# Reordering the hand-written end of the attention and giving the 1024-wide weights a fifth flag

## The reference

```python
x = x + attn(layernorm(x))
x = x + xattn(layernorm(x), ctx, ctx, mask)
h = silu(h_in @ w1.T * s1) * (h_in @ w2.T * s2)      # h_in = layernorm(x), 256 -> 1024
h = gelu(h @ h1.T * s_h1)                            # 1024 -> 1024
h = gelu(h @ h2.T * s_h2)                            # 1024 -> 1024
x = x + h @ w3.T * s3                                # 1024 -> 256
```

## Time and profile before

| What | Value |
|---|---|
| median of 3 runs | 1508.51 us (1506.88 to 1509.42) |
| profiled execution, its own time | 1507.81 us |
| its span in the trace | 1506.0 us |
| mean granted TensorE clock | 0.999 |
| PE busy | 1487.9 us, 99% |
| DVE, ACT, POOL busy | 1101.3, 968.6, 492.1 us |

### The profile page before, as it was taken

The page is one execution under the profiler, slowest core; times in us unless marked ns, Lnnn a source line. Parts: engine busy times, 40 slices in busy tenths (PEclk is TensorE's granted clock), DMA queues, the critical chain, the costliest instruction groups (busy, mean ns, idle before and its releaser), DMA issues.

```text
span 1506.0 us, 29162 instructions
## 1 busy us (share of the span) xinstructions
PE 1487.9 (99%) x10680; PEld 1262.7 (84%) x10680; DVE 1101.3 (73%) x2772; ACT 968.6 (64%) x2274; POOL 492.1 (33%) x763
## 2 busy tenths in 40 slices
PE   8999999999999999999998999999999999999999
PEld 6888888888888888888887788888888888888887
DVE  7999999999999899999999657555553634444443
ACT  6888888888888888888887754456444532222222
POOL 2545454445544555454453011000110212221110
PEclk9999999999999999999999999999999999999999
DMA  4000000000000000000013423421212632222221
GB/s 155 2 1 2 30 2 30 1 2 30 2 29 1 2 30 1 16 15 2 22 64 113 145 84 113 150 103 66 79 66 78 215 114 85 84 85 84 85 84 43
DMA packets 56024, 87.15 MB, mean 58 GB/s; under 512 B 4416, under 2 KB 33472, under 8 KB 55872
## 3 DMA queue, kind: packets, MB, share of 16 engines
q1 hardware_dynamic: 55872, 85.10, 16.5%
HBM read 55.72 MB, written 29.36 MB: 56 GB/s over the span
## 4 chain that ended last, share of the span: by engine, by line
PE 91%; DVE 5%; ACT 2%; DMA 1%; issue 1%; POOL 0%; SPq 0%; DVEq 0%
PE bank L1024 15%; PE bank L1026 13%; PE bank L658 10%; PE bank L578 9%; PE bank L630 8%; PE bank L580 7%; PE bank L579 7%; PE bank L642 6%; PE bank L1179 2%; PE bank L1170 2%; PE bank L1032 2%; PE bank L1146 2%; PE bank L1138 2%; PE bank L1139 2%; PE bank L1140 2%
## 5 line engine op out<-in xcount | busy, mean ns | idle before, releaser
L844 POOL TENSOR_SCALAR P<-P,stats 128x512 f32<-128x512 f32 (+3 forms) x512 | 269.0, 544 | 376.4 <-DVE stats L822 376.1
L717 ACT ACTIVATE P<-P,stats 128x384 f32<-128x384 f32 (+3 forms) x512 | 283.9, 560 | 16.4 <-DVE stats L814 16.2
L681 ACT ACTIVATE PT<-bank 128x512 fp32r<-128x512 f32 (+1 forms) x384 | 185.4, 525 | 87.6 <-PE bank L642 86.5
L814 DVE CUSTOM_DVE_ANT_0 P<-bank,cmask 128x384 f32<-128x384 f32 (+3 forms) x512 | 228.4, 483 | 1.2 <-PE bank L630 0.9
L731 DVE TENSOR_TENSOR PT<-bank,PT 128x512 fp32r<-128x512 f32 (+1 forms) x384 | 218.8, 594 | 5.3 <-ACT PT L681 4.1
L1336 DVE TENSOR_TENSOR Hb<-gt,Hb 128x512 fp32r<-128x512 f32 x128 | 90.8, 710 | 167.0 <-ACT Hb L1187 165.9
L1024 PE MATMUL bank<-Hb,hw 128*128 128x512 f32 x512 | 202.3, 395 | 0.8 <-DVE Hb L1336 0.8
L1024 PE MATMUL bank<-w,hw 128*128 128x512 f32 x512 | 199.2, 389 | 0.0
L658 PEld LDWEIGHTS bank<-PT,V 128*128 128x128 f32 x1024 | 165.0, 190 | 22.1 <-DVE PT L731 4.3
L658 PE MATMUL bank<-PT,V 128*128 128x512 f32 (+3 forms) x1024 | 176.7, 320 | 3.5 <-DVE PT L731 3.5
L1026 PE MATMUL bank<-Hb,hw 128*128 128x512 f32 x448 | 174.8, 390 | 0.0
(11 more groups left out here) (230 smaller groups left out, 3305.4 us busy)
## 6 DMA issues: line engine op xcount, KB each, us to landing
h_scratch<-go SPq DMA_DIRECT2D x64, 256.0 KB, 2.0
xs<-x_scratch SPq DMA_DIRECT2D x23, 512.0 KB, 4.1
hx<-h_scratch SPq DMA_DIRECT2D x32, 256.0 KB, 6.1
stageA<-in_h SPq DMA_DIRECT2D x14, 512.0 KB, 3.6
x_scratch<-x SPq DMA_DIRECT2D x8, 512.0 KB, 3.0
x_scratch<-xs SPq DMA_DIRECT2D x8, 512.0 KB, 2.9
qf<-h_scratch SPq DMA_DIRECT2D x16, 256.0 KB, 5.3
pf<-h_scratch SPq DMA_DIRECT2D x16, 256.0 KB, 6.0
```

Source lines behind the costliest of these rows:

```text
L681: return e.activation(dst, src, ACT.Copy, scale=scale)
L717: e.activation(p, p, ACT.Exp, bias=st_[:, k:k + 1], scale=-1.0, accum_out=st_[:, 8 + k:9 + k]).then_inc(s_exp, 1)
L814: e.tensor_tensor_reduce(P_tile(P, i, a), banks["S", P, max(i, 1)][a][:, slice(*S_COLS[i])], cmask[:, 512 - n:512], -1.0, 3.0e38, ALU.add, ...
L844: e.tensor_scalar(p, p, stats[P % 4][:, k:k + 1], 1.0, ALU.mult, ALU.mult).then_inc(s_norm, 1)
```

## The change

- In TAIL the ends of the five lists are reordered. PE does `g.0.0` to `u.0.2` ahead of `O.63` and `O.64`. DVE does `pl.63.2.0` and `os.62` ahead of `xoa`, `lnorm.1.0` earlier, and `fl.12` after `hl.0.7`. ACT does `big.12` and `fh.13` to `fh.16` after `hh.0.7`. SP issues `xload.1` after `ld.9` and `ld.14` after `ld.12`.
- There is a flag 4. Flag 3 covers pieces 5 to 10, flag 4 pieces 5 to 12 and is loaded in `h.0.2`; `ft.4` and `fm.4` follow `h.0.1`.
- The row of flag 2 is transposed and loaded after the first three matmuls of both `g.0.0` and `u.0.0`; their last matmuls follow then.
- A gated tile waits for the high parts of XTs ahead of its first two matmuls, for the first low part ahead of the third, and for the second low part ahead of the fourth.

```diff
 "PE"
-        T.63.1 O.62 xo.0.0 xo.0.1 AV.63.0 AV.63.1 xv.2 xv.3 xt.0.1.0 xt.0.1.1 ft.2 O.63 O.64 g.0.0 u.0.0 g.0.1
-        u.0.1 g.0.2 u.0.2 g.0.3 u.0.3 g.0.4 u.0.4 g.0.5 u.0.5 g.0.6 u.0.6 g.0.7 u.0.7 ft.3""",
+        T.63.1 O.62 xo.0.0 xo.0.1 AV.63.0 AV.63.1 xv.2 xv.3 xt.0.1.0 xt.0.1.1 ft.2 g.0.0 u.0.0 g.0.1 u.0.1 g.0.2
+        u.0.2 O.63 O.64 g.0.3 u.0.3 g.0.4 u.0.4 g.0.5 u.0.5 g.0.6 u.0.6 g.0.7 u.0.7 ft.3""",
 "ACT"
-        ph.63.0.1 ph.63.1.0 ph.63.1.1 ph.63.2.0 fh.7 fh.8 big.7 yo.63.0 fh.9 yo.63.1 big.8 xvh.2 fh.10 xvh.3
-        xth.0.1.0 xth.0.1.1 big.9 fh.11 big.10 silu.0.0 silu.0.1 big.11 silu.0.2 hh.0.1 silu.0.3 hh.0.3 silu.0.4
-        fh.12 silu.0.5 fh.13 fh.14 big.12 hh.0.5 silu.0.6 silu.0.7 fh.15 hh.0.6 hh.0.7 fh.16 big.13 big.14""",
+        ph.63.0.1 ph.63.1.0 ph.63.1.1 ph.63.2.0 fh.7 fh.8 yo.63.0 yo.63.1 fh.9 big.7 xth.0.1.0 xth.0.1.1 big.8
+        xvh.2 silu.0.0 xvh.3 fh.10 silu.0.1 big.9 silu.0.2 hh.0.1 fh.11 silu.0.3 big.10 hh.0.3 silu.0.4 silu.0.5
+        hh.0.5 big.11 silu.0.6 fh.12 silu.0.7 hh.0.6 hh.0.7 big.12 fh.13 fh.14 fh.15 fh.16 big.13 big.14""",
 "DVE"
-        xvl.1 xr.0 ys.62.1 pl.63.0.0 pl.63.2.1 xpl.0 pl.63.0.1 pl.63.1.0 pl.63.1.1 xoa.0.0 os.62 fl.7 pl.63.2.0
-        xoa.0.1 lsum.0.1 ys.63.0 fl.8 xva.2 ys.63.1 lnorm.0.1 xva.3 flag.2 fl.9 xtl.0.1.0 xtl.0.1.1 fl.10 fm.2
-        fl.11 xvl.2 xvl.3 os.63 os.64 hm.0.0 hm.0.1 hl.0.0 hm.0.2 hl.0.1 hm.0.3 hl.0.2 hl.0.3 hm.0.4 fl.12
-        hl.0.4 hm.0.5 lsum.1.0 flag.3 hl.0.5 fm.3 hm.0.6 hm.0.7 lnorm.1.0 hl.0.6 hl.0.7 fl.13 fl.14 fl.15 fl.16""",
+        xvl.1 xr.0 ys.62.1 pl.63.0.0 pl.63.2.1 xpl.0 pl.63.0.1 pl.63.1.0 pl.63.1.1 pl.63.2.0 os.62 xoa.0.0
+        xoa.0.1 lsum.0.1 fl.7 ys.63.0 lnorm.0.1 fl.8 xtl.0.1.0 xtl.0.1.1 xva.2 flag.2 xva.3 fm.2 ys.63.1 fl.9
+        hm.0.0 xvl.2 xvl.3 hm.0.1 hl.0.0 fl.10 hm.0.2 hl.0.1 os.63 os.64 lsum.1.0 hm.0.3 hl.0.2 hl.0.3 fl.11
+        hm.0.4 hl.0.4 hm.0.5 lnorm.1.0 hl.0.5 flag.3 fm.3 hm.0.6 hl.0.6 hm.0.7 hl.0.7 fl.12 flag.4 fl.13 fl.14
+        fl.15 fl.16""",
 "POOL"
-        n.63.1.0 yh.62 yl.62 lpow.0.1 yh.63 yl.63 hh.0.0 hh.0.2 hh.0.4 lpow.1.0""",
+        n.63.1.0 yh.62 yl.62 lpow.0.1 yh.63 yl.63 hh.0.0 hh.0.2 lpow.1.0 hh.0.4""",
 "SP"
-        xload.0 st.6 mb ld.0 ld.1 ld.2 ld.3 ld.6 ld.5 ld.4 ld.7 ld.8 ld.9 ld.10 ld.11 ld.13 ld.14 st.7 ld.12
-        ld.15 xload.1 ld.16""",
+        xload.0 st.6 mb ld.0 ld.1 ld.2 ld.3 ld.6 ld.5 ld.4 ld.7 ld.8 ld.9 xload.1 ld.10 ld.11 ld.13 st.7 ld.12
+        ld.14 ld.15 ld.16""",
...
-                o += [("h", 0, 1)] + also(0, ("h", 1)) + [("gelu", 0, 1), ("hst", 0, 1), ("big", 16)]
+                o += [("h", 0, 1), ("ft", 4), ("fm", 4)] + also(0, ("h", 1)) + [("gelu", 0, 1), ("hst", 0, 1), ("big", 16)]
...
-    FLAGS = (2, 3, 0, 1)
-    LOOKED = {2: 4, 3: 8, 0: 12}
+    FLAGS = (2, 3, 4, 0, 1)
+    LOOKED = {2: 4, 3: 6, 4: 8, 0: 12}
...
+        def gated(kind, m, out, ready):
+
+            W, ms = w1 if kind == "g" else w2, slice(m * 128, m * 128 + 128)
+            w.wait_ge(s_x2hi, ready)
+            e.matmul(out[:, :], W[:, 0, 0, ms], XTs[:, 0, 0, :], start=True, stop=False)
+            e.matmul(out[:, :], W[:, 0, 1, ms], XTs[:, 0, 1, :], start=False, stop=False)
+            w.wait_ge(s_x2lo, ready - 1)
+            e.matmul(out[:, :], W[:, 0, 0, ms], XTs[:, 1, 0, :], start=False, stop=False)
+
+        def gated_rest(kind, m, out, ready):
+            W, ms = w1 if kind == "g" else w2, slice(m * 128, m * 128 + 128)
+            with e.If_ne(low, 0):
+                for c in range(2):
+                    e.matmul(out[:, :], W[:, 1, c, ms], XTs[:, 0, c, :], start=False, stop=False)
+            w.wait_ge(s_x2lo, ready)
+            e.matmul(out[:, :], W[:, 0, 1, ms], XTs[:, 1, 1, :], start=False, stop=True).then_inc(s_gu, 1)
...
-                if item == ("g", 0, 0):
-                    look_up(2)
...
+                gated(kind, m, out, xt_at(b, 1))
+                if item == ("u", 0, 0):
+                    flag_row(2)
+                    look_up(2)
+                    gated_rest("g", m, bank["g", 0, 0], xt_at(b, 1))
+                if item != ("g", 0, 0):
+                    gated_rest(kind, m, out, xt_at(b, 1))
...
-                       {(0, 0): 3, (0, 4): 0}.get((b, m)), ...
+                       {(0, 0): 3, (0, 2): 4, (0, 4): 0}.get((b, m)), ...
```

More of the change, by code:

```diff
@@ L356, in program @@
     st = at(1.21875, "st0", [128, 12])
-    flags = at(1.28125, "flags", [128, 8])
+    flags = at(1.28125, "flags", [128, 10])
     rmax = [at(1.375 + 0.0625 * i, f"rmax{i}", [128, 16]) for i in range(2)]
@@ L1008, in look_up, with flag_row @@
             e.reg_load(low, flags[0:1, 2 * k + 1:2 * k + 2].bitcast(i32))
+        def flag_row(k):
+            out, = claim(w, ("ft", k))
+            w.wait_ge(s_found, FLAGS.index(k) + 1)
+            e.transpose(out[0:1, 0:128], flags[:, 2 * k:2 * k + 1], ident[:, :]).then_inc(s_ft, 1)
+        def gated(kind, m, out, ready):
[12 more added lines that the diff above has]
+            e.matmul(out[:, :], W[:, 0, 1, ms], XTs[:, 1, 1, :], start=False, stop=True).then_inc(s_gu, 1)
         def scores_by_rows(b):
@@ L1123, in pe_rest @@
                 i.then_inc(s_xo, 1)
[L1124 to L1127, removed]
+            elif kind == "ft" and a[0] != 2:
+                flag_row(a[0])
             elif kind == "use":
@@ L1131, in pe_rest @@
                 b, m = a
-                ms = slice(m * 128, m * 128 + 128)
                 out, = claim(w, item)
[L1134 to L1140, removed]
-                if item == ("g", 0, 0):
+                for q in split_done(W1 if kind == "g" else W2):
+                    w.wait_ge(*q)
+                gated(kind, m, out, xt_at(b, 1))
+                if item == ("u", 0, 0):
+                    flag_row(2)
                     look_up(2)
[L1143 to L1146, removed]
+                    gated_rest("g", m, bank["g", 0, 0], xt_at(b, 1))
+                if item != ("g", 0, 0):
+                    gated_rest(kind, m, out, xt_at(b, 1))
             elif kind == "h":
@@ L1153, in pe_rest @@
                 hidden(out, lambda i, c: Hb[c][:, i, :], m, lambda c: (s_hlo, 8 * b + c + 1),
-                       {(0, 0): 3, (0, 4): 0}.get((b, m)), b + 1 if m == (2 if b == 0 else 1) and b + 1 < B else 0).then_inc(s_hid, 1)
+                       {(0, 0): 3, (0, 2): 4, (0, 4): 0}.get((b, m)), b + 1 if m == (2 if b == 0 else 1) and b + 1 < B else 0).then_inc(s_hid, 1)
             elif kind == "gh":
```

## The result

Five executions of each kernel on one chip: 1514.77 us (median; 1514.64 to 1516.89) after, 1506.88 us (1506.43 to 1509.42) before; ratio 1.0051 [1.0036, 1.0065]. The change makes the kernel slower, by 7.9 us between the medians. The profiled execution of after took 1516.89 us with a span of 1515.1. The forecast of 1514.6 lies closer to the median than its sum does: it was 6.1 us on top of 1508.51, the median of three, and five executions put before at 1506.88. That it hits the median within 0.2 us is luck: the base was 1.6 us too high and the sum 1.8 too low.

What follows compares the result with a forecast made beforehand. PE, busy 99% of the span, was taken to bound the kernel. Terms of +4.5 (xs.1), +0.3 (look-up), +1.8 (half clock) and -0.5 (wait) gave +6.1 us, 1514.6 as a median; range 1509.5 to 1519.

Steps and rivals of the forecast that it cites:

- Steps 1 and 2: Handover and first gated tiles: xt 4.2 us early, g.0.0 at 815.7, then 1.3 us lost at flag 2's row.
- step 1: Handover from AV.63 to xt: AV.63 starts 2.5 us earlier at full clock, and xt starts 4.2 us early.
- Step 3: At ft.3, which waits for flag.3 on DVE: ft.3 comes at 836.5, 1.5 us early.
- Step 4: From ft.3 to xs.1: ACT's and DVE's chain takes 16.3 us, so PE waits about 5.5 us ahead of xs.1.
- Step 5: The rest: look-up 0.3 us, half clock at the xs.1 gap 1.8, a later wait of 0.5 gone.
- The look-up in h.0.2: Loading the new flag within h.0.2 costs 0.3 us, as the one in h.0.0 did.
- The 0.5 us wait of the earlier trace: PE's largest wait after 857 us goes, as later batches' gated tiles start on the high parts: 0.5 us gained.
- The sum: Whole kernel: +4.5 at xs.1, +0.3 look-up, +1.8 half clock, -0.5 wait, together 6.1 us slower.
- That ACT catches up: Rival at xs.1: xtl.1.0.1 ends before about 847.5, so the kernel is about 3 us faster, 1505.3; chance 0.14.
- No change: Rival: the gap ahead of xs.1 is half as long and the clock stays up, +1 to +3 us; chance 0.14.
- That the clock falls in the handover too: Rival: gaps from 812.3 to 818.5 bring another half clock, another 1.8 us partly hidden, 1516; chance 0.12.

Runs made afterwards that it cites:

- e2_late: The kernel after with ACT's and DVE's weight pieces 12 to 14 and lnorm.1.0 put about where before had them; 1510.05 us, ratio to before 1.0012.
- e3_code: All five lists of the kernel before with the code of the kernel after, flag.4 the only item added; 1507.41 us, ratio to before 0.9997.
- b6: b2 with the flag's register load moved two steps earlier in the hidden tile; 1504.32 us, ratio to before 0.9975.
- b3: The kernel before, its code, flags and PE list kept, with ACT's, DVE's and SP's lists reordered; 1507.16 us, ratio to before 0.9993.
- d1_pieces: The kernel after with fh.13 and fh.14 moved ahead of big.12 on ACT; 1515.4 us, ratio to before 1.0052.
- d2_sums: d1_pieces with big.13 and big.14 moved ahead of fh.16 on ACT; 1515.47 us, ratio to before 1.0045.
- e1_warm: The kernel after plus unused PE transposes, 36 ahead of xs.1 and 20 ahead of ft.3; 1512.82 us, ratio to before 1.0032.
- e4_early: The kernel before, code and PE list kept, with the handover's items moved early on ACT and DVE alone; 1509.76 us, ratio to before 1.0012.
- b2: The kernel after, code and PE list kept, with ACT's and DVE's lists reordered in another order than b1; 1506.57 us, ratio to before 0.999.
- b5: b1 with the flag's register load moved two steps earlier in the hidden tile; 1505.61 us, ratio to before 0.9981.
- e5_late_warm: e2_late with 30 unused PE transposes ahead of ft.3; 1510.09 us, ratio to before 1.0014.
- b1: The kernel after, code and PE list kept, with ACT's and DVE's lists reordered and xload.1 moved on SP; 1506.06 us, ratio to before 0.9986.

## Why the prediction was right, and where it was off

**Right: the direction and the mechanism.** The forecast was that the handover gains some 4 us which are lost again at ft.3, and that xs.1 then waits for ACT and DVE, whose lists put pieces 12 to 16 too late. That is what the trace shows (5.28 us of wait where PE was to be 5.5 ahead), and e2_late, which moves these items and little else, takes that wait away.

**Steps 1 and 2, right within 0.4 us.** Less the 1.72 of the start: AV.63 805.9, xt.0.1 813.57 (forecast 813.9), g.0.0 815.49 (815.7), PE goes on at 818.54 (818.5), the gap 1.31 (1.3). The terms of step 1 add up to 814.0, not 813.9; lpow took 1.93 us, between its bound of 1.46 and the 2.58 in the sum.

**Step 3, off by 1.4 us: ft.3 came at 837.94, not 836.5.** DVE's work ahead of flag.3 was counted nearly right (20.6 us, measured 20.98) and its waits were not: they were put at some 2 us. A window of DVE from the end of lnorm.0.1 to flag.3 (us, DVE busy, PEclk, DMA share, GB/s) has 3.2 us of them:

```profile
815.20:839.40 24.20, 20.98 (x42) 1.00 0.37 129
```

The largest, 1.66 us ahead of hm.0.0, was on no list. hm.0.0 needs silu.0.0, and ahead of its first silu ACT loads the table of that function. In after ACT waits for g.0.0 there, and the load starts only when that wait is over. ACT's and DVE's timeline of after:

```profile
820.82 1.28 ACT L1300 ACT_TABLE_LOAD   x1 [2.14 <-PE bank L1032]
```

```profile
822.90 0.75 DVE L1498 SCALAR_TENSOR_TENSOR gt<-bank,s1c,gt 128x512 f32<-128x512 f32 x1 [1.66 <-PE bank L1032]
```

The row names a matmul that had ended by 821.1; what ended last was silu.0.0, at 822.81. So the load's 1.28 us stand in the chain, ahead of hm.0.0. Before had the same load (at 823.65), but DVE had os.63 and os.64 to do until 825.2, and hm.0.0 waited 0.51 us. DVE's timeline of before:

```profile
825.73 1.42 DVE L1481 SCALAR_TENSOR_TENSOR gt<-bank,s1c,gt 128x512 f32<-128x512 f32 x2 [0.51 <-PE bank L1146]
```

No run has the load elsewhere, so that all of it would come back at ft.3 is argued, not shown. The low end that the step kept (834.8, DVE without a wait) was the wrong side to look at. That two pieces fewer save nothing was right for before's lists (e3_code, the same 0.81 us wait). In b6 the flag is served ahead of piece 12, and b3, without the fifth flag, waits 2.09 us there; these two differ in more than the flag (b3's late load above all), so what it is worth alone isn't shown.

**Step 4, right term by term.** From ft.3 to xs.1 it is 16.23 us, against 16.3 to 16.4. The step had fh.13 to fh.15 (3.0 us) beside the load of piece 16 and the load ending 0.6 us later; the load took 3.79 us, not 3.5, and fh.16 waited 0.99 for it. d1_pieces confirms which of the two ends last. One sign of this step didn't come: PE has no gap of over 1 us ahead of step 7 of h.0.0, because the half clock held it back until DVE was there. The chain of waits of after, in order of time (start, us, what):

```profile
846.79 0.20 ACT stageC L1220
847.00 3.79 DMA stageC<-in_h
850.84 0.93 issue
851.77 1.13 ACT go L1220 x2
```

The 0.93 us that the chain calls issue are fh.16. The rest of the sum holds as well: big.12 starts 6.17 us after ft.3, where fm.3, the tiles' items and fl.12 were to take 6.4. The two sums that stand between fh.16 and xth.1.0 were worth 1.3 of their 2.3 us when d2_sums took them away.

**Step 5, the clock.** One phase of half clock was forecast, at 1.8 us with bounds 0 and 3.6. There were two; the one that counts cost 2.0 (e1_warm), the other nothing. That the clock falls in the wait ahead of xs.1 was right; that it would also fall behind the shorter one at ft.3 stood only in the upper bound, which priced it at 1.8. The look-up in h.0.2 was put at 0.3, and no run has it by itself: e3_code's trace has 1.1 us for all of the new code, and its times show no difference. The 0.5 us wait of the earlier trace rows is gone, as forecast: the longest wait of PE behind xs.1 is 0.2 us.

**The sum:** 6.1 us forecast, 7.4 in the traces. xs.1 is 1.3 later than forecast (1.4 from step 3, 0.1 back from step 4); what lies behind xs.1 was forecast within 0.1 (1.6 both), though 2.0 of it is the clock and -0.4 the rest, where the forecast had 1.8 and -0.2. Differences of that size are within the scatter.

**The rivals.** That ACT catches up: no, xth.1.0 started at 852.1 (853.85 less 1.72), and xtl.1.0.1 had to end by 847.5. No change: outside of the interval; flag.3 was later than forecast, not earlier, and the wait at xs.1 of full length. That the clock falls in the handover too: not in after, where the gaps there are 1.31 us at most; it did in e4_early, whose gaps were 2.86 and 2.00. ft.3 itself lies outside of its stated 834.8 to 836.6. The signs that hang on it came about 1.1 late with it: big.12 at 844.1 (near 843), xth.1.0 at 852.1 (near 851).

**Left open:** which of the moves in b6 gives how much, how much of b3's miss is the flag, how much of the sum is left to gain by an earlier table load, and whether b2's loss was the slow register load in all of its executions; none of these was run by itself.

## What to carry to other kernels

An order written by hand is judged where its last item is next needed: list, for each engine, what stands ahead of the next item that PE waits for, and include the loads that these items release; a buffer freed late puts a whole load into the chain (3.8 us here), and work beside that load is free (1.9 us of it in d1_pieces). A slow phase of the clock costs time only where PE sets the pace, so fill the wait in front of such a stretch or remove it, and leave the others. A register load in the middle of a tile is worth moving where its engine has work queued or would wait anyway (b6), but look first at what PE waits for next: in b5 that took nearly all of the gain.

## What the runs showed of the hardware that was not expected

- A register load of one number on PE takes 0.30 us in most cases and 0.49 at times; the longest took 0.91 us in e2_late, 0.86 in e5_late_warm, 1.73 in b1 and 1.69 in b2. Moved ahead two steps (b5, b6) the longest took 0.481 and 0.485. What makes it slow isn't shown.
- The same half clock is free or dear: 6.8 us of it cost nothing (e2_late against e5_late_warm), another 6.8 us cost 2.0 (after against e1_warm).
- The table load of the first silu starts only when the wait ahead of it is over, in each trace that has such a wait: 0.44 us of idle time in before, 2.14 in after and e1_warm, 2.10 in e3_code, 1.52 in e4_early, 0.74 in b6. In none of them was it hidden in that wait.
- One load of 512 KB, issued from the same place of the same list, landed after 3.57 us in one trace and 5.05 in another.
- DVE's four normalising instructions on 128x256 took 2.82 to 2.84 us beside POOL's two on 128x512 (before, e3_code, e4_early) and 1.37 to 1.38 us without them (after, b3, b6).
